# The last self attention of a six-stage decoder kernel: dense query and key projections, and scores as three fp32r products on 32-row strips

## What is computed

```
h = rmsnorm(X, norm1_w)
q = (h @ wq).reshape(B, S, N_HEADS, D_HEAD)
k = (h @ wk).reshape(B, S, N_HEADS, D_HEAD)
v = (h @ wv).reshape(B, S, N_HEADS, D_HEAD)
scores = jnp.einsum('bshd,bthd->bhst', q, k) * scale
attn = jax.nn.softmax(scores, axis=-1)
ctx = jnp.einsum('bhst,bthd->bshd', attn, v).reshape(B, S, d)
X = X + ctx @ wo
h2 = rmsnorm(X, norm2_w).reshape(B * S, d)
```

## Time and profile before

| | us |
|---|---|
| three runs | 2158.28, 2162.51, 2163.05 |
| median | 2162.51 |
| span of the profiled execution | 2165.8 |
| PE busy in it | 1867.8 (86%) |
| DVE busy | 1203.0 (56%) |
| ACT busy | 995.9 (46%) |
| POOL busy | 676.3 (31%) |
| the stretch 1560 to 1820 of this stage: PE, DVE, ACT, POOL busy | 232.19, 166.44, 106.74, 21.08 |

### The profile page before, as it was taken

The page is one execution under the profiler, slowest core; times in us unless marked ns, Lnnn a source line. Parts: engine busy times, 40 slices in busy tenths (PEclk is TensorE's granted clock), DMA queues, the critical chain, the costliest instruction groups (busy, mean ns, idle before and its releaser), DMA issues. The chain is left out here.

```text
span 2165.8 us, 41835 instructions
## 1 busy us (share of the span) xinstructions
PE 1867.8 (86%) x15764; PEld 1450.1 (67%) x15764; DVE 1203.0 (56%) x2996; ACT 995.9 (46%) x2350; POOL 676.3 (31%) x609
## 2 busy tenths in 40 slices
PE   7888875999579999499999995899599896899994
PEld 5676764676368988367777774666366564788884
DVE  3666654676445554445555554466466664447774
ACT  5656542453234454445555552444244342346663
POOL 2434334685223323233233333111101000243443
PEclk9999987998579999799999999899599997999997
DMA  2000002010235434310000000100103103823334
GB/s 65 11 11 21 12 11 71 2 31 11 96 135 153 111 123 126 106 57 2 11 14 18 11 6 29 41 23 20 57 2 121 39 12 101 307 95 52 53 53 100
DMA packets 97870, 125.52 MB, mean 58 GB/s; under 512 B 8554, under 2 KB 84794, under 8 KB 97642
## 3 DMA queue, kind: packets, MB, share of 16 engines
q1 hardware_dynamic: 84378, 105.07, 14.7%
q0 software_dynamic: 13296, 17.77, 4.7%
HBM read 85.02 MB, written 39.89 MB: 58 GB/s over the span
## 5 line engine op out<-in xcount | busy, mean ns | idle before, releaser
L2116 POOL TENSOR_TENSOR L1a_probs<-L1a_probs,L1a_rinv 128x1024 f32<-128x1024 f32 x64 | 121.2, 1893 | 269.3 <-DVE L1a_rinv L2431 269.3
L2113 POOL TENSOR_TENSOR L0a_probs<-L0a_probs,L0a_rinv 128x256 f32<-128x256 f32 (+1 forms) x128 | 103.1, 826 | 189.7 <-DVE L0a_rinv L2431 189.7
L2423 DVE CUSTOM_DVE_ANT_0 L1a_sbias<-L1a_psS,L1a_bias 128x256 f32<-128x256 f32 x256 | 93.3, 420 | 108.2 <-PE L1a_psS L2224 108.2
L2376 ACT ACTIVATE L1a_probs<-L1a_sbias,L1a_nmx 128x256 f32<-128x256 f32 x256 | 126.8, 498 | 46.7 <-DVE L1a_nmx L2423 46.6
L2376 ACT ACTIVATE L0a_probs<-L0a_sbias,L0a_nmx 128x128 f32<-128x128 f32 (+1 forms) x256 | 113.1, 444 | 28.7 <-DVE L0a_nmx L2423 28.7
L3103 POOL DMA_INDIRECT moe_sums<-moe_y,moe_xg x39 | 82.0, 2101 | 136.2 <-DVE moe_y L3402 117.3
L2687 POOL DMA_INDIRECT ec_sums<-ec_yk,ec_token_at x32 | 59.0, 1844 | 190.4 <-ACT ec_yk L2808 185.5
L1647 ACT ACTIVATE L1s_pT<-L1s_psK 128x1024 f32<-128x1024 f32 x64 | 65.6, 1025 | 99.0 <-PE L1s_psK L1521 99.0
L2873 DVE TENSOR_TENSOR ec_h<-ec_sg,ec_psU 128x512 f32<-128x512 f32 x64 | 44.0, 687 | 119.9 <-ACT ec_sg L2795 119.9
L3181 PE MATMUL moe_psY<-moe_wts,moe_hT 128*128 (+1 forms) x440 | 104.0, 379 | 0.8 <-ACT moe_hT L3248 0.8
L1794 DVE TENSOR_REDUCE L1s_top<-L1s_psS 128x4 f32<-128x1024 f32 x64 | 78.4, 1226 | 44.1 <-PE L1s_psS L1506 44.0
(11 more groups left out here) (525 smaller groups left out, 5006.3 us busy)
## 6 DMA issues: line engine op xcount, KB each, us to landing
shelf<-in_L_ffn_w_gate SPq DMA_DIRECT2D x8, 1024.0 KB, 9.2
shelf<-in_L_ffn_w_up SPq DMA_DIRECT2D x8, 1024.0 KB, 12.9
ec_wd<-in_L_ffn_w_down SPq DMA_DIRECT2D x8, 1024.0 KB, 6.3
moe_rows<-blank SPq DMA_DIRECT2D x1, 5070.0 KB, 19.5
moe_xg<-moe_rows SPq DMA_DIRECT2D x39, 130.0 KB, 2.1
moe_wts<-in_L_ffn_e_gate SPq DMA_DIRECT2D x8, 512.0 KB, 9.9
moe_wts<-in_L_ffn_e_up SPq DMA_DIRECT2D x8, 512.0 KB, 9.8
moe_wts<-in_L_ffn_e_down SPq DMA_DIRECT2D x8, 512.0 KB, 9.9
```

Of the source, the lines that this page charges most:

```text
L2113: last = pool.tensor_tensor(v, v, bcast(rinv[:, r, :, t], 2, KEYS[t]), ALU.mult)
L2116: last = pool.tensor_tensor(v, v, bcast(rinv[:, r, :, :].rearrange("p h t -> p (h t)"), 2, S), ALU.mult)
L2376: ins = act.activation(probs[:, r, j, at], sbias[:, g % 2, j, at], ACT.Exp, bias=nmx[:, r, j, t:t + 1], scale=-1.0, accum_out=sums[:, r, j ...
L2423: last = dve.tensor_tensor_reduce(out=sbias[:, g % 2, j, at], in0=psS[:, slot + j, at], in1=added, scale=-1.0, scalar=LARGE, op0=ALU.add, ...
```

## The change

`narrow_stage` becomes `self_stage`, for this kind only; branches for other kinds, which no caller used, go away. In what runs:

- Query and key projections are dense. An item now gives 128 columns of queries and 128 of keys, eight heads at once, two per strip of 32 partitions; there are two such items a batch (o = 0, 1) and not four. They stand in (0,1) and (1,1) of the plan, and v moves from (1,1) to (3,0). The first batch computes xT, qk 0, qk 1 and v before its first scores.
- Each set st is now the even or odd head of every strip (par = st % 2) of item o = st // 2. Queries are kept as high and low part for each par, with the other head's rows multiplied by zero (`half` holds 0.25 or 0 per partition). Keys are kept as a high part, and as a low part `km` per par, in which the other head's rows are zero except one row of ones (`one`, `others`).
- S and K are each three fp32r products in place of one fp32 product.
- Taking a qk item is three ACT activations of 128x256 (two with a factor per partition), then three DVE operations of 128x256, then two POOL operations of 128x256 (`mark_keys`), which come in POOL's order ahead of root_front in st = 1, and ahead of root in st = 2. S of a set waits for `k_marked`.
- The shifted queries go to a tile of their own, `shifted`, in place of being written over the queries.
- The weight split is one activation and one subtraction for each of q and k, in place of eight activations and sixteen DVE operations; zeroing of the padded weights and the setting of the constant row go, six small DVE operations that make the masks come.

No transfer of SP is added, removed or moved. The core of the diff:

```diff
-            PLAN = {(0, 0): (("xT", 1),), (0, 1): (("qk", 1, 0),), (1, 0): (("qk", 1, 1),), (1, 1): (("v", 1),),
-                    (2, 0): (("out", -1),), (2, 1): (("qk", 1, 2),), (3, 0): (("qk", 1, 3),)}
+        FRONT = (("xT",), ("qk", 0), ("qk", 1), ("v",))
+        FRONT_HOMES = {("qk", 1): psK[:, 0, :], ("v",): psO[:]}
+        PLAN = {(0, 0): (("xT", 1),), (0, 1): (("qk", 1, 0),), (1, 1): (("qk", 1, 1),),
+                (2, 0): (("out", -1),), (3, 0): (("v", 1),)}
...
         @block.gpsimd
+            def mark_keys(b, o):
+
+                wait_taken(pool, ("qk", o), b)
+                if b >= 2:
+                    pool.wait_ge(k_ready, 2 * (NST * (b - 2) + 2 * o + 1) + 2)
+                for par in range(2):
+                    pool.tensor_scalar(km[:, b % 2, o, par, :], kl[:, o, :], others[:, par:par + 1], one[:, par:par + 1],
+                                       ALU.mult, ALU.add).then_inc(k_marked, 1)
...
             for n in range(N):
                 b, st = divmod(n, NST)
+                if b + 1 < B and st in (1, 2):
+                    mark_keys(b + 1, st - 1)
...
         @block.tensor
                 elif what[0] == "qk":
-                    st = what[1]
                     pe.wait_ge(w_ready, 2)
-                    terms(ps[:, 0:S], [(lambda a, c=c: wqk[:, a, c, 0, st, :, :].rearrange("p j e -> p (j e)"),
-                                         lambda a, c=c: xT[:, a, c, :]) for c in range(KD)])
...
+                    for j in range(2):
+                        cols = slice(j * D + what[1] * P, j * D + (what[1] + 1) * P)
+                        last = terms(ps[:, j * S:(j + 1) * S], [(lambda a, c=c: wqk[:, a, c, cols],
+                                                                 lambda a, c=c: xT[:, a, c, :]) for c in range(KD)])
...
             def scores_part(n, pair, t):
-                b, st = divmod(n, NST)
-                for j in (2 * pair, 2 * pair + 1):
-                    r = slice(32 * j, 32 * j + 32)
-                    last = pe.matmul(psS[:, j, t * KEYS:(t + 1) * KEYS], qk[r, b % 2, st, t * P:(t + 1) * P],
-                                     qk[r, b % 2, st, S:QK], start=True, stop=True)
+                at = slice(t * P, (t + 1) * P)
+                for k in range(3):
+                    for j in (2 * pair, 2 * pair + 1):
+                        high, low, keys, marked = parts(n, slice(32 * j, 32 * j + 32))
+                        l, r = ((high, keys), (low, keys), (high, marked))[k]
+                        last = pe.matmul(psS[:, j, t * S:(t + 1) * S], l[:, at], r, start=(k == 0), stop=(k == 2))
                 return last
...
             def turned_part(n, half, kt):
+                at = slice(kt * P, (kt + 1) * P)
+                for k in range(3):
+                    for jj in range(2):
+                        rows = slice(64 * half + 32 * jj, 64 * half + 32 * jj + 32)
+                        high, low, keys, marked = parts(n, rows)
+                        l, r = ((keys, high), (keys, low), (marked, shifted[rows, n % 2, :]))[k]
+                        last = pe.matmul(psK[:, jj, kt * S:(kt + 1) * S], l[:, at], r, start=(k == 0), stop=(k == 2))
...
         @block.scalar
                 elif what[0] == "qk":
-                    act.activation(qk[:, b % 2, what[1], :], ps[:, 0:QK], ACT.Identity, bias=row16[:, 0:1]).then_inc(sm, 1)
+                    for par in range(2):
+                        act.activation(qs[:, b % 2, o, 0, par, :], ps[:, 0:S], ACT.Copy, scale=half[:, par:par + 1])
+                    act.activation(kh[:, b % 2, o, :], ps[:, S:2 * S], ACT.Copy).then_inc(item_high, 1)
...
         @block.vector
+                elif what[0] == "qk":
+                    dve.wait_ge(item_high, HIGHS[what, b] + 1)
...
+                    for par in range(2):
+                        dve.scalar_tensor_tensor(out=qs[:, b % 2, o, 1, par, :], in0=ps[:, 0:S], scalar=half[:, par:par + 1],
+                                                 in1=qs[:, b % 2, o, 0, par, :], op0=ALU.mult, op1=ALU.subtract)
+                    dve.tensor_tensor(kl[:, o, :], ps[:, S:2 * S], kh[:, b % 2, o, :], ALU.subtract).then_inc(item_taken, 1)
...
-                dve.tensor_tensor(q, bank(("top",), n)[:, 0:S], q, ALU.add).then_inc(q_shifted, 1)
+                dve.tensor_tensor(shifted[:, n % 2, :], psF[:, 0:S], qs[:, b % 2, st // 2, 0, st % 2, :], ALU.add)\
+                    .then_inc(q_shifted, 1)
```

## The result

The changed kernel took 2192.84 us (median of 4 runs, 2188.95 to 2195.52), the kernel before 2162.78 us (4 runs beside it, 2158.28 to 2169.19): ratio **1.014** (95% interval 1.0117 to 1.0164), 30 us slower.

The account below looks back on a forecast made before the run. TensorE bounds a 30.82 us batch; new waits lengthen it. 3.2 + 5 x 4.94 + 2.3 + 1 - 5.1 + 7.5 = +33.6 us on 2162.5 gives 2196 us; 8 in 10: 2170 to 2218.

Parts of the forecast that it names:

- The chain: Item, ScalarE, VectorE, b+2 statistics, GpSimd root and low part: out item 9.55 us behind its block, TensorE waiting 4.3.
- The two later waits: Later in each batch TensorE waits for row maxima: 1.4 us behind output statistics, 1.3 behind the first query/key item.
- The block: Joint S and K score block on TensorE: 1.31 us instead of 1.08, bounds 0.91 and 1.63, eight per batch.
- The clock: Granted TensorE clock falls to 0.5 behind long waits: 6 x 1.25 = +7.5 us, bounds 0 and 10.
- The rival of full overlap: Joint blocks: all four strips always overlap, blocks 0.91 us; with no clock loss +14, 2176 us; chance 0.10.
- The rivals for "faster": Out item's start: as early as now, 5.5 us instead of 9.55, waits hidden, 2147 or 2125 us; chance 0.11.
- if only that chain broke: Out item no longer late, other waits stay: batch 32.7 us, whole +11, 2173 us; no separate chance given.
- TensorE's sum would decide: Out item early and smaller waits hidden: -15 us, 2147, or 2125 with overlapping strips; under faster, chance 0.11.
- The store stall: Batch 3, VectorE's wait for a store behind the 5 MB blanking transfer: hidden by longer batches, -5.1 us.
- Front and end: Stage edges: later first scores, two fewer projection items, four edge blocks; +1 us, bounds -2 to +4.

Follow-up runs that it names:

- e1: Changed kernel with the statistics of batch b+2 on VectorE issued ahead of taking the second query/key item; ratio 1.0012 to the kernel before.
- e2: Changed kernel with GpSimd's low part of the head outputs issued ahead of the root of the input statistics; ratio 1.0046 to the kernel before.
- e6: Kernel before, with VectorE's statistics of batch b+2 made to wait until ScalarE has emptied the value item; ratio 1.0081 to the kernel before.
- e4: Changed kernel with all twelve S matmuls of a joint block written ahead of all twelve K; ratio 1.0213 to the kernel before.
- e9: e8 with the low parts of queries and keys put behind the statistics of b+2; ratio 0.9924 to the kernel before.
- e10: e9 with the blanking transfer of batch 1 issued behind that batch's two stores; ratio 0.9888 to the kernel before.
- e8: Changed kernel with early query/key bank copy, high and low parts made later, GpSimd's output low part earlier, output statistics one row maximum later; ratio 0.996 to before.

## Why the prediction was right, and where it wasn't

The time, 2196 us against 2192.8, came out of the right mechanism, two wrong sizes that largely cancelled, and some luck. I worked out the differences from the trace of before, and between the two traces the change costs 22.9 us, not 33.6: 5 us less than forecast in the seven stretches (242.7 against 240.2 + 7.5) and 5.8 less outside them. That the medians differ by 30.1 is the distance of the two profiled executions from their medians, which I had no part in.

- **The chain: right.** ScalarE 1.11 us (taken 1.12), VectorE 1.20 (1.2), out item 9.11 us behind its block (9.55), a wait of 4.57 us (4.3), five times. The two later waits are there, 1.9 and 1.74 us (1.4 and 1.3). e1, e2 and e6 show it from three sides: taken apart at either end the loss goes, put into the kernel before it costs the delay in full.
- **The block: the step that failed.** "The rounds where one group ends and the next begins are shared, three of twelve" gave 1.31 us; all rounds are shared, 0.92, the lower bound that I worked out as 0.91. The Trainium skill, "TensorE: Matmul & The Clock Gate", "Part 3: Packing small matmuls", says that matmuls start in strict program order; I let that decide between my two ends. The trace disagrees: a K matmul starts 0.02 us behind the first S, past four earlier ones, and in e4 past six. By the rule the block would have stayed at 1.31. A batch has eight blocks, so TensorE's work was oversized by 3.1 us a batch. At full clock the batches' TensorE busy time is 24.3 us (e9), against 28.65 before: the change saves 4.3 us of work per batch, not 1.4.
- **The clock: undersized.** I charged 7.5 us for six falls, at most 10. There are eleven. TensorE's busy times in the seven stretches sum to 184.5 us; in e10, with the same matmuls and all seven stretches at 1.00, they sum to 166.4. So 18 us of TensorE's time in this stage is the same instructions at the lower clock. I counted only waits of over 3 us; e8 shows it behind 1.93 us, and the changed kernel behind the waits for the maxima too (1.92 us, and 1.74 at 1790.56 with a fall at 1791.48).
- **The two together.** My batches summed, without the clock, to 240.2 us; measured less those 18 they are 224.6. Some 16 us too much for blocks and what follows from them, some 11 too little for the clock. The rival of full overlap, at 2176, had the block right and assumed no clock loss at all; that assumption is what failed it. The two effects should have been separate terms. (This takes all of the 18 us as lying on the path.)
- **The rivals for "faster"**: "if only that chain broke", 2173 us, was tried in e1, which comes to 1.0012 of 2162.8, 2165. "TensorE's sum would decide" gave 2147 us with blocks of 1.31 and 2125 with the overlap that the trace shows. e9 comes to 0.9924, 2146, and its nearness to 2147 is chance: there a batch of 28.1 us still has 3.8 us of waiting (before: 2.2), and batch 3 its store stall, so TensorE's sum does not yet decide.
- **The store stall: right.** The 5.1 us it took in batch 3 are hidden by the longer batches; e9 shows it coming back, with 7.2 us of wait, once they are short.
- **Front and end**: I took +1; the rest of the stage and the program came out 4.8 us shorter, of which 2.3 lie ahead of the stage's first matmul and so are no effect of the change.

## What to carry to other kernels

When an item moves to another place, ask not only who takes it but what stands behind the taking on that engine, and behind that on the next: here an item's evacuation (2.3 us, and the wait for the item itself) delayed a statistic that nobody needed for a batch, this delayed a root, and the root a low part that TensorE was waiting for. Off-path work with a late due time goes behind on-path work in every in-order queue. And a TensorE stall is priced twice, as the wait and as the slower clock behind it: a fall cost 1.5 us here, and falls came behind waits from 1.74 us up, though not behind each.

## What the runs showed of the hardware

- Matmuls on different 32-row strips overlap out of program order: blocks of 0.91 and 0.92 us, whether S and K are written alternating or six by six. They do so over a limited distance: with twelve S ahead, the first K waited until six of them were left (block 1.26 us).
- Single-pass fp32r matmuls of 32x256 on a strip follow each other every 0.12 us, four strips at once, with their weight loads beside them.
- Waits of 1.1 us before the out items of five batches left the clock at 1.00 in e10 (and in e9, but for batch 3 with its stall of 5.7 us); waits of 1.93 us in e8 were followed by falls in four batches of five, and the first of them by none. In e1 waits of 1.74 us were followed by falls in some batches and not in others. What decides between these was not tried.
- A delay of 2.2 us in each of five batches that adds no work (e6) cost 0.8% of the whole program.
